# A state-space recurrence in a fused layer: D u moved to ScalarE, dt kept doubled, a small buffer for the normalised rows, new banks and a new slot table

## What is computed

```
xz = x @ in_proj_w.T;  xc, z = split(xz)
u  = conv4(xc) + conv_b                      # 4 taps, 512 -> 512 channels
dt = clip(sigmoid(u @ dt_w.T + dt_b), 1e-4, 1.0)
A  = -exp(A_log);  Bm = u @ B_w.T;  Cm = u @ C_w.T   # 16 states
for t in range(512):
    dA = exp(clip(dt * A, -5, 5))
    state = dA * state + dt * Bm * u + 1e-6
    y[t] = sum(state * Cm, states) + D * u
return (y * silu(z)) @ out_w.T
```

## Time and profile before

| what | us |
|---|---|
| three runs, median (lowest to highest) | 1505.53 (1499.43 to 1505.67) |
| the profiled execution's own time | 1496.55 |
| its span, first to last instruction | 1494.8 |
| first scan of the recurrence starts | 474.25 |
| batch 4 of the recurrence, from its first scan to that of batch 5 | 102.7 |

### The profile page before, as it was taken

One profiled execution on the slowest core, in us unless ns is written; L12 is line 12 of the kernel. 1 busy time (PEld: TensorE's weight loads), 2 busy tenths in 40 slices (PEclk: granted clock), 3 DMA queues, 4 the chain that ended last, 5 costly groups with the idle time before them and its releaser, 6 DMA issues.

```text
span 1494.8 us, 22147 instructions
## 1 busy us (share of the span) xinstructions
PE 1379.2 (92%) x6998; PEld 965.2 (65%) x6998; DVE 1034.4 (69%) x1557; ACT 951.9 (64%) x1765; POOL 849.1 (57%) x412
## 2 busy tenths in 40 slices
PE   5899999999998988989989989999899888889997
PEld 2566696999744555555655655555556676569996
DVE  6666615333333899998899989998998997853332
...
GB/s 300 79 28 28 29 86 137 212 207 210 157 49 16 148 225 161 201 222 159 210 222 154 209 213 170 217 172 203 218 149 208 209 198 212 77 239 209 211 209 82
DMA packets 108231, 248.40 MB, mean 166 GB/s; under 512 B 19098, under 2 KB 49951, under 8 KB 94049
## 3 DMA queue, kind: packets, MB, share of 16 engines
...
q10 hardware_dynamic: 2080, 1.47, 0.3%
...
## 4 chain that ended last, share of the span: by engine, by line
PE 63%; DVE 12%; ACT 11%; issue 8%; DMA 4%; POOL 1%; DVEq 0%; POOLq 0%; ACTq 0%; SPq 0%
PE ps L1534 11%; PE ps L1269 10%; PE ps L1474 9%; PE ps L1483 9%; PE ps L1565 4%; DVE arena L1166 4%; ACT arena L710 4%; ACT arena L720 4%; PE ps L1294 4%; PE ps L1331 2%; PE ps L1285 2%; PE ps L1610 2%; PE ps L1419 2%; PE ps L1389 2%; DVE x L1166 1%
## 5 line engine op out<-in xcount | busy, mean ns | idle before, releaser
L485 POOL TENSOR_TENSOR arena<-arena 128x2048 f32<-128x2048 f32 x97 | 445.6, 4594 | 150.6 <-DVE arena L1166 140.3
L1166 DVE TENSOR_TENSOR_SCAN arena<-arena,ps 128x512 f32<-128x512 f32 x392 | 471.5, 1212 | 64.0 <-PE ps L1269 54.3
L1269 PEld LDWEIGHTS ps<-cst,arena 128*128 128x128 f32 x2428 | 308.0, 148 | 310.1 <-issue 197.8
L1269 PE MATMUL ps<-cst,arena 128*128 128x128 f32 x2428 | 380.7, 285 | 72.4 <-ACT arena L720 34.0
L710 ACT ACTIVATE arena<-arena,a_neg 128x512 f32<-128x512 f32 x512 | 366.4, 716 | 47.9 <-DVE arena L1166 36.4
L720 ACT ACTIVATE arena<-arena,m_bt 128x512 f32<-128x512 f32 x512 | 363.4, 710 | 2.8 <-DVE arena L1097 1.7
L1534 PE MATMUL ps<-arena,tapw 128*128 128x512 f32 x512 | 259.1, 606 | 0.3 <-ACT arena L669 0.3
L1042 DVE TENSOR_TENSOR arena<-ps,arena 128x256 f32<-128x256 f32 x78 | 33.2, 425 | 201.0 <-PE ps L1483 197.9
L453 POOL DMA_INDIRECT arena<-rows,arena x78 | 75.8, 972 | 166.1 <-DVE arena L1022 143.0
L1166 DVE TENSOR_TENSOR_SCAN x<-arena,ps 128x512 f32<-128x512 f32 x120 | 144.0, 1211 | 19.0 <-PE ps L1269 16.4
L1474 PEld LDWEIGHTS ps<-arena 128*128 128x128 f32 x1248 | 153.3, 194 | 4.6 <-ACT arena L618 0.5
...
## 6 DMA issues: line engine op xcount, KB each, us to landing
...
arena<-c_rows SPq DMA_DIRECT2D x128, 256.0 KB, 3.8
...
```

Source lines behind the costliest of these rows:

```text
L485: g.tensor_tensor(h, h, m_c[i % RC].unsqueeze(1).to_broadcast([P, KI, SEQ]), ALU.mult)\
L1166: v.tensor_tensor_scan(out=h[:, k, :], data0=m_a[g % RA], data1=ps[SCAN_BANK[g % 3]][:, :], initial=0.0, op0=ALU.mult, op1=ALU.add).then_i ...
L1269: return t.transpose(bank, src[:, k * P:(k + 1) * P], ident)
```

## The change

- D·u: `m_skip` moves from DVE to ACT, which copies u with scale D into the bank of y. The sums and products of y use three banks, `Y_BANK` (4, 5, 7, 4) in place of (4, 5, 4, 5), in another order of slots.
- dt is kept doubled: ACT stops after tanh, `m_clip` adds 1 and takes the maximum with 2e-4, `a_neg` is -exp(A_log)/2, and `m_weigh` multiplies by 0.5 in its one instruction.
- The normalised rows go through two slices in the buffer `m_bc` of B and C: `m_norm` of block 2 and 3 waits until PE has turned the block two before. PE turns a block at a time (two transposes each) at four slots, `XT_AT`. The first waits for the store of C rows (`m_cst`), which SP now issues in the middle of a batch (`C_STORE`).
- z goes to the banks of the output, 4 and 5 twice, in place of 7, 0, 7, 1.
- The slot tables are written anew.

```diff
+XN = 2
-UT_AT = (9, 17, 24, 34)
+UT_AT = (12, 18, 25, 33)
-DTT_AT = (40, 44, 50, 55)
+DTT_AT = (41, 42, 51, 55)
-NORM_AT = (52, 53, 55, 57)
+NORM_AT = (44, 50, 52, 58)
-SKIP_AT = (44, 50, 14, 15)
+SKIP_AT = (3, 5, 10, 16)
...
+        m_xn = m_bc.rearrange("p (c d) -> p c d", c=XN)
...
+                    if n == C_STORE and b < BATCH - 1:
+                        store_c(b + 1)
...
             def m_norm(n, c):
                 if c == 0:
                     a.wait_ge(S("m_stat0"), min(n, 1) + 1)
-                    if n >= 2:
-                        a.wait_ge(S("m_y0"), KI * (n - 2) + 2)
+                    if n:
+                        a.wait_ge(S("m_cst"), 16 * n)
+                        a.wait_ge(S("m_btr"), n)
...
+                if c >= XN:
+                    a.wait_ge(S("m_xct"), CPB * n + c - XN + 1)
...
                 a.activation(dt, dt, ACT.Tanh, bias=mvec[:, 1, o:o + 1], scale=0.5).then_inc(S("m_th"), 1)
-                a.wait_ge(S("m_th"), KI * n + o + 1)
-                a.activation(dt, dt, ACT.Copy, bias=0.5, scale=0.5).then_inc(S("m_dt0"), 1)
...
+            def m_skip(b, k):
+
+                if k < 2:
+                    a.wait_ge(S("m_sz"), KI * (b + 1))
...
+                if k == 3:
+                    a.wait_ge(S("m_y"), KI * b + 1)
+                a.activation(ps[Y_BANK[k]][:, :], m_u[b % 2][:, k, :], ACT.Copy, scale=mvec[:, 2, k:k + 1])\
+                    .then_inc(S("m_y0"), 1)
...
-                if o == 2:
-                    for c in range(CPB):
-                        m_norm(1, c)
...
+            for c in range(XN):
+                m_norm(1, c)
+            for c in range(CPB):
+                m_input(0, c)
+            for c in range(XN, CPB):
+                m_norm(1, c)
             for k in range(KD):
                 m_xtcopy(1, k)
-            for c in range(CPB):
-                m_input(0, c)
...
-                v.wait_ge(S("m_dt0"), KI * n + o + 1)
-                v.tensor_scalar(m_dt[n % 2][:, o, :], dt_bank(n, o)[:, :], 1e-4, 1.0, ALU.max, ALU.min).then_inc(S("m_dt1"), 1)
+                v.wait_ge(S("m_th"), KI * n + o + 1)
+                v.tensor_scalar(m_dt[n % 2][:, o, :], dt_bank(n, o)[:, :], 1.0, 2e-4, ALU.add, ALU.max).then_inc(S("m_dt1"), 1)
...
-                v.tensor_scalar(ps[4 + k % 2][:, :], m_u[b % 2][:, k, :], mvec[:, 2, k:k + 1], None, ALU.mult)\
-                    .then_inc(S("m_y0"), 1)
...
-            def m_turn(n, k):
-
-                if k == 0:
-                    t.wait_ge(S("m_xn"), CPB * (n + 1))
+            def m_turn(n, c):
+
+                t.wait_ge(S("m_xn"), CPB * n + c + 1)
...
+                if n >= 2 and c == 0:
+                    t.wait_ge(S("m_wt"), KI * (n - 1) + 3)
+                for k in range(KD):
+                    last = turned(ps[XT_BANK[k]][:, c * P:(c + 1) * P], m_xn[:, c % XN, :], k, c)
...
                 if b < BATCH - 1 and k == 0:
-                    if o == 0 and b:
-                        t.wait_ge(S("m_sz"), KI * b)
-                    if o == 0:
-                        t.wait_ge(S("m_btc"), b + 2)
-                    if o == 1:
-                        t.wait_ge(S("m_wt"), KI * (b + 1) + 3)
-                    if o == 2:
-                        t.wait_ge(S("m_sz"), KI * b + 1)
-                    if o == 3:
-                        t.wait_ge(S("m_wt"), KI * (b + 1) + 4)
+                    if o < 2 and b:
+                        t.wait_ge(S("m_xupd"), 2 * (b - 1) + o + 1)
+                    if o < 2 and not b:
+                        t.wait_ge(S("m_wt"), KI)
+                    if o >= 2:
+                        t.wait_ge(S("m_sz"), KI * b + o - 1)
```

More of the change, by code:

```diff
@@ L771, in _ @@
                         m_input(g // KI + 1, q % KI)
+                    if b and q in SKIP_AT:
+                        m_skip(b - 1, SKIP_AT.index(q))
                     if b < BATCH - 1:
@@ L1530, in m_conv @@
                     t.wait_ge(S("m_xtc"), KD * n + 2)
+                if o == 1 and i == 0 and n >= 2:
+                    t.wait_ge(S("m_wt"), KI * n)
                 if o >= 2 and i == 0:
@@ L1644, in m_prep @@
                     m_bturn(n)
-                for k in range(KD):
-                    if n < BATCH - 1 and q == XT_AT[k]:
-                        m_turn(n + 1, k)
+                for c in range(CPB):
+                    if n < BATCH - 1 and q == XT_AT[c]:
+                        m_turn(n + 1, c)
             def m_late(b, q):
```

146 lines of the change are left out of this document (73 added, 73 removed).

## The result

The kernel after takes 1489.65 us (median of 16 runs, 1486.68 to 1494.34), the kernel before 1497.05 (16 runs, 1490.93 to 1505.67). The ratio is 0.9942, 95% interval [0.9925, 0.9958]: 8.7 us less (6.3 to 11.2), where the two medians alone differ by 7.4. A later reading of the unchanged kernel gave 0.9933 [0.9908, 0.9959]. The forecast was 12.8 us less. The 1493 us were taken from a first median of 1505.5, which was high; the difference is what can be judged.

What follows compares the result with a forecast made beforehand. A relay of busy engines was taken to bound a middle batch: PE, DVE, PE, ACT. Six middle batches at 1.94 us (11.6) and batch 7's 1.2 gave 12.8 off 1505.5, so 1493 us; range 1481 to 1505.

Steps and rivals of the forecast that it cites:

- within 0.5%: Whole kernel: time changes by less than 7.5 us, hardly told from no change; chance 26%.
- ACT, slots 46 to 64: Middle batches: two copies and one normalised block leave the stretch that ACT fills, gaining 1.47 us a batch.
- z's banks: Slots 46 to 64: changed waits worth nothing, but DVE may wait for the later z tanh, costing 0.3 us a batch.
- DVE, slots 8 to 22: Two D·u leave the stretch where DVE is the busy engine, gaining 1.2 us a batch; 0 at the low end.
- PE, slots 22 to 46: One more output product falls in the stretch where PE is the busy engine, costing 0.43 us a batch.
- D·u on ACT, slots 0 to 22: Four D·u of 0.62 us each come to ACT, covered by its spare time: nothing, or 0.1 us.
- The small buffer: Normalised rows in the B/C buffer: waits for turns and the C store are met in time, costing nothing.
- the loop at slots 48 to 53: Rival, the slower case: clip, transpose, weigh, turn and third block wait on each other; 7.5 us slower, 1513; chance 12%.
- The start: Ahead of the first scan: two normalised blocks and a turn now stand behind the inputs, costing 1.3 us once.
- batch 7 gains only the 1.2: Last batch: it prepares no other batch, so it gains only the 1.2 us of slots 8 to 22.
- PE holds it: Rival: PE's dense slots 15 to 19 hold the scans, the 1.2 us falls away, 1501 or 1505 us; chance 26%.
- More than the sum: Rival: new banks keep PE going at full clock, 3.9 us a batch in all, 1481 us; chance 17%.

Runs made afterwards that it cites:

- e1: Kernel before with only dt kept doubled, so no ACT copy behind the tanh; 1493.10 us, ratio to before 0.9998.
- e6: Kernel after with the tanh copies back on ACT and dt not doubled; 1483.58 us, ratio to before 0.9930.
- e11: Kernel after with four PE waits of the kernel before put back, two on z products and two on turns; 1500.72 us, ratio to before 0.9988.
- e9: Kernel after with the first normalised block at slot 48 in place of 44; 1486.74 us, ratio to before 0.9938.
- e2: Kernel after with D·u back on DVE at the same slots; 1483.91 us, ratio to before 0.9932.
- e7: Kernel after with three unread filler products per batch on PE, at slots 62 and 63; 1476.95 us, ratio to before 0.9874.
- e4: Kernel after with the second batch's normalised rows in the buffer of u, turned before the inputs; 1481.28 us, ratio to before 0.9916.
- e5: Kernel after with two late loads of the last batch issued one step earlier; 1479.83 us, ratio to before 0.9875.
- e3: Kernel after with the last three products of the second convolution group at slots 11 to 13; 1482.14 us, ratio to before 0.9925.
- e8: Kernel after with the second and third groups of convolution products earlier; 1479.43 us, ratio to before 0.9889.

## Why the prediction was right, and where it was not

**In all.** Faster by 0.58%, inside the range; 8.7 us (10.0 by the second reading) against 12.8. The interval of the ratio, 0.42 to 0.75%, does not quite exclude the case "within 0.5%". The middle batches gave 10.98 of the 11.6, but out of other terms than I gave them: 1.65 us less a batch behind slot 46 and 0.71 less in slots 8 to 46, where I had 1.17 and 0.77, and 0.53 more in slots 0 to 8, where I had nothing. That 1.83 lies so near to 1.94 is luck. Start and batch 7 took the rest.

**ACT, slots 46 to 64 (1.47 forecast), and z's banks (−0.3 forecast).** Together 1.17; measured 1.65. Here a step failed: "ACT fills it to 28.87 of 28.93 us", therefore its work is the bound. The busy time of the whole stretch hid where the limit lies. In parts, mean of batches 1 to 6, in us:

| slots | before | e1 | after | e6 | e11 |
|---|---|---|---|---|---|
| 46–52 | 9.11 | 9.11 | 9.06 | 9.06 | 9.06 |
| 52–56 | 6.29 | 6.29 | 5.62 | 6.16 | 5.62 |
| 56–58 | 4.30 | 4.72 | 3.42 | 3.42 | 3.42 |
| 58–62 | 5.92 | 5.83 | 6.27 | 6.27 | 6.27 |
| 62–64 | 3.02 | 2.87 | 2.62 | 2.63 | 3.61 |

In the kernel before, DVE has no pause up to the scan of slot 56, so ACT's work there is worth nothing (e1). The 0.67 in slots 52 to 56 are two statistics of the layer norm on DVE, which `STAT_AT` moves from slots 52 and 54 to 58 and 63, where they cost 0.35 and 0.31: nothing in all. The gain lies behind them.

- *Slots 62 to 64, 0.71 us: the turns' wait for the last gate.* The wait exists because z lay in the banks that the turned rows share. I had read it, 2.10 us, and costed it at nothing because PE "idles there already". Batch 6 turns no rows and takes 2.25 us there in the kernel before; batches 1 and 2 take 3.49, so the wait costs 1.24, with the half clock that begins behind it (the mean granted clock of slot 63 of batch 1 is 0.73). With it put back, e11 is 1.19 longer in the mean of batches 1 to 5, all in these slots; its other three waits lengthen nothing. In batches 3 to 5 of the kernel before the wait costs 0.56 to 0.84, since the slots ahead are already late there. (The 0.71 is the mean of six, with the moved statistic set apart.)
- *Slots 56 to 58, 0.88 us: TensorE's clock.* In all six batches of the kernel before PE waits 1.8 us for ACT's inputs and DVE's first gate ahead of the third z product, whose first half stands at slot 56. In batches 1 and 2 the clock stays at full and slots 56 and 57 take 3.45 us; in batches 3 to 6 it falls behind the wait, and they take 4.72; in e1 it falls in all six. The new `Z_AT` has both halves at slot 57, PE waits for nothing there, and all six batches take 3.42 at full clock. Slots 56 and 57 of batches 1 and 4 before, and of batch 4 after:

```profile
661.18:664.63 3.45, 3.31 (x14) 1.97 (x15) 3.45 (x5) 3.45 (x7) 3.45 (x1) 1.00 1.02 245
969.07:973.79 4.72, 4.58 (x13) 2.65 (x14) 3.60 (x5) 4.72 (x10) 4.42 (x2) 0.64 1.02 235
```
```profile
963.51:966.93 3.42, 2.44 (x9) 1.17 (x8) 3.42 (x6) 3.42 (x7) 3.42 (x2) 1.00 1.04 263
```

That half clock costs these slots 1.27 us is read from equal waits at either level; that the move of the product took it away is argued from the traces, and no run moves the product alone. The 0.55 of e6 is a price in the kernel after, in slots whose gain was DVE's; that 1.00 + 0.55 comes near to 1.65 says nothing. The block moved out gives about 0.1 (e9), not 0.49.

**DVE, slots 8 to 22 (1.2), and PE, slots 22 to 46 (−0.43).** Together −0.77 us; measured 24.70 + 37.24 to 24.23 + 37.00, −0.71. The sum is right and both terms are wrong. PE's limit begins at slot 16, not 22. Batch 4 from slot 8 to 16 and from 16 to 46, before and after:

```profile
891.73:906.18 14.45, 14.45 (x67) 8.26 (x66) 14.03 (x17) 12.37 (x20) 10.45 (x4) 1.00 0.42 113
906.18:953.67 47.49, 46.12 (x221) 28.28 (x220) 42.77 (x46) 43.56 (x71) 40.82 (x15) 1.00 0.93 204
```
```profile
887.59:902.32 14.73, 13.92 (x62) 7.87 (x61) 14.38 (x18) 13.48 (x23) 10.39 (x4) 1.00 0.42 108
902.32:948.82 46.50, 46.50 (x226) 28.68 (x225) 40.41 (x42) 42.97 (x70) 41.00 (x15) 1.00 0.98 208
```

The added output product is there, 46.12 to 46.50 us of PE work. But 1.37 us of PE's idle time between slots 16 and 46 are gone. In the kernel before they were two waits, ahead of the transposes of slot 20 and of the first output product:

```profile
910.52 0.66 PE L1269 MATMUL ps<-cst,arena 128*128 128x128 f32 x4 [0.72 <-ACT arena L720]
916.57 0.70 PE L1610 MATMUL ps<-outw,arena 128*128 128x256 f32 x2 [0.64 <-DVE arena L1128]
```

Slots 8 to 16 are 0.28 longer. The D·u themselves are worth 0.25 (e2); the rest, some 0.46, came with the slot table. That PE's dense slots hold the scans was my lower bound for this term, and the 0.94 us wait at slot 20 is that.

**D·u on ACT, slots 0 to 22 (nothing).** One takes 0.61 us (890.34 to 890.95), forecast 0.62:

```profile
890.34 0.67 ACT L719 ACTIVATE ps<-arena,mvec 128x512 f32<-128x512 f32 x1
890.95 0.67 ACT L682 ACTIVATE arena<-ps,mvec 128x512 f32<-128x512 f32 x1
```

ACT has idle time around them, and slots 8 to 22 are no longer for them. At full clock slots 0 to 8 are not longer either: the shortest are 11.24 us before and 11.23 after. Right. The Trainium skill (VectorE: DVE Perf Modes, the TRN2 errata) has ScalarE pay more for a source in SBUF than for one in PSUM; the trace agrees in sign, 0.61 against 0.49 for the copy within PSUM.

**Slots 0 to 8 (nothing).** Measured +0.53 a batch (11.81 to 12.34, in both traces of the kernel after), 3.2 us in six: TensorE's half clock behind the batch change, up to 13.76 us, against at most 12.38 before. With the idle time filled they take 11.28 (e7). That the change would cost clock here is a term that the forecast lacked.

**The small buffer (nothing), the loop at slots 48 to 53.** No idle time of ACT ahead of a block in the middle batches, and slots 46 to 52 take 9.06 us against 9.11. Right.

**The start (−1.3).** Measured −1.41, shown by e4. Right.

**Batch 0 (about 0 with the start) and batch 7 (a gain of 1.2).** With the start counted apart, batch 0 was to gain 1.17 us and gained 2.39; but it takes 95.9 to 98.1 us in the traces with the changed tables (98.35 before), so one trace each does not size it. Batch 7 did gain its 1.67 us in slots 8 to 22 and lost 1.61 in all, 0.95 of it in slots 0 to 8. The failed step is "batch 7 gains only the 1.2": it takes a gain ahead of a wait for a gain. The turn at slot 34 waits for a transfer, so time won before it is given back there. e5 shows that the wait goes when the transfer is issued earlier. It is not the place alone: with the loads unchanged the slot took 3.51 us in e2 and 1.74 in e7.

**The rivals.** "PE holds it" was right on the mechanism (e2, e3, e8) and wrong on its price. "More than the sum" named the clock at the batch change: slots 0 to 8 take 12.34 us where 11.28 is possible (e7), so 1.06 a batch stayed unclaimed. In slots 56 and 57 its mechanism did come and gave 0.88 in the mean; in slots 0 to 8 the clock took 0.53 back, and the expected 3.9 a batch did not come. Nothing of the slower case, the loop, was seen.
